# Newton steps of three inverse square roots moved from GpSimd to VectorE, in a fused graph-attention and transformer kernel

## The reference, cut to what matters

```python
x = x + gat(gat(ctx_512, adj=layernorm(x)))      # 8 heads of 32, leaky relu, masked softmax, elu
```

```python
hidden = layernorm(x)
h = rmsnorm(hidden, attn_norm_w)
q, k, v = h @ q_w.T, h @ k_w.T, h @ v_w.T        # 16 query heads, 4 key/value heads of 128
q, k = rope(rmsnorm(q, q_norm_w)), rope(rmsnorm(k, k_norm_w))
hidden = hidden + causal_attention(q, k, v) @ o_w.T
h2 = rmsnorm(hidden, ffn_norm_w)                 # then 8 experts of 176, top 2 by softmax(h2 @ gate_w.T)
out = x + hidden + sum_e combine_e * (silu(h2 @ wg_e.T) * (h2 @ wu_e.T)) @ wd_e.T
```

## Time and profile before

| what | us |
|---|---|
| median of 3 runs (lowest to highest) | 663.96 (662.97 to 664.13) |
| the profiled execution | 662.46 |
| its span | 660.7 |
| TensorE busy | 606.6 (92%) |
| VectorE busy | 434.6 (66%) |
| GpSimd busy | 305.9 (46%) |
| ScalarE busy | 268.6 (41%) |

### The profile page before, as it was taken

One profiled execution on the slowest core, in us unless ns is written; L12 is line 12 of the kernel. 1 busy time (PEld: TensorE's weight loads), 2 busy tenths in 40 slices (PEclk: granted clock), 3 DMA queues, 4 the chain that ended last, 5 costly groups with the idle time before them and its releaser, 6 DMA issues.

```text
span 660.7 us, 10362 instructions
## 1 busy us (share of the span) xinstructions
PE 606.6 (92%) x3271; PEld 437.0 (66%) x3271; DVE 434.6 (66%) x1279; ACT 268.6 (41%) x653; POOL 305.9 (46%) x588
## 2 busy tenths in 40 slices
PE   3799899489799999989799999989999998999998
PEld 2278468236586789736597789746768873666886
DVE  4997499389756387689757387655653656664463
ACT  2462563065566333055556333036750204675020
POOL 1493594278853240268854150267730027863000
PEclk9999899799999999998989999999999999999999
DMA  8920000000000000000000000000000000000000
GB/s 276 387 73 2 1 1 4 12 4 2 1 1 0 1 2 1 24 9 1 0 2 1 0 1 1 3 15 1 1 1 0 1 9 8 1 0 1 1 0 17
DMA packets 8729, 14.41 MB, mean 22 GB/s; under 512 B 908, under 2 KB 7372, under 8 KB 8420
## 3 DMA queue, kind: packets, MB, share of 16 engines
q1 hardware_dynamic: 8676, 13.76, 5.9%
HBM read 12.70 MB, written 1.05 MB: 21 GB/s over the span
## 4 chain that ended last, share of the span: by engine, by line
PE 64%; DVE 20%; issue 6%; POOL 4%; ACT 4%; DMA 1%; DVEq 0%; POOLq 0%; SPq 0%; ACTq 0%
PE bank L615 14%; PE bank L513 10%; PE bank L573 6%; PE bank L559 5%; PE bank L592 4%; PE ob L487 4%; PE tb L476 3%; PE bank L637 2%; DVE tt L958 2%; PE bank L588 2%; PE bank L584 2%; DVE ssq L1023 2%; ACT prob L726 2%; DVE m L1020 2%; DVE qT L958 1%
## 5 line engine op out<-in xcount | busy, mean ns | idle before, releaser
L559 PE MATMUL bank<-wqkv_sb,hT 128*128 128x512 f32 x192 | 95.0, 635 | 0.4 <-ACT v_sb L702 0.4
L726 ACT ACTIVATE prob<-bank,sneg,rms 128x128 f32<-128x128 f32 (+1 forms) x128 | 63.9, 508 | 59.6 <-DVE sneg L1052 59.4
L836 POOL TENSOR_TENSOR m<-early,rope_s 128x256 f32<-128x256 f32 x80 | 73.5, 942 | 30.8 <-ACT early L707 30.6
L513 PE MATMUL bank<-m,wgu_sb 128*128 128x128 f32 (+1 forms) x480 | 85.6, 329 | 0.8 <-DVE early L1099 0.8
L794 POOL TENSOR_SCALAR tt<-tt,gmn 128x256 f32<-128x256 f32 x96 | 67.3, 710 | 37.4 <-DVE gmn L958 37.0
L852 POOL TENSOR_SCALAR prob<-prob,srcp 128x128 f32<-128x128 f32 (+1 forms) x128 | 53.1, 432 | 51.4 <-DVE srcp L1123 51.2
L513 PEld LDWEIGHTS bank<-m,wgu_sb 128*128 128x128 f32 x480 | 71.0, 191 | 9.0 <-DVE early L1099 2.2
L573 PE MATMUL bank<-kT,qT 128*128 128x128 f32 (+1 forms) x256 | 61.5, 356 | 1.8 <-ACT prob L726 1.8
L559 PEld LDWEIGHTS bank<-wqkv_sb,hT 128*128 128x128 f32 x192 | 35.9, 199 | 36.9 <-issue 34.0
L615 PE MATMUL bank<-wo_sb,qT 128*128 128x256 f32 x256 | 59.0, 382 | 0.7 <-ACT qT L732 0.7
L707 ACT ACTIVATE early<-bank 128x512 f32<-128x512 f32 x40 | 24.1, 602 | 84.4 <-PE bank L559 84.4
(11 more groups left out here) (200 smaller groups left out, 1217.0 us busy)
## 6 DMA issues: line engine op xcount, KB each, us to landing
wqkv_sb<-wqkv_dram SPq DMA_DIRECT2D x1, 3072.0 KB, 12.0
wgu_sb<-wgu_dram SPq DMA_DIRECT2D x2, 1408.0 KB, 11.5
wo_sb<-wo_dram SPq DMA_DIRECT2D x1, 2048.0 KB, 18.2
wd_sb<-wd_dram SPq DMA_DIRECT2D x1, 1408.0 KB, 15.6
out_dram<-rows SPq DMA_DIRECT2D x8, 128.0 KB, 1.7
xin<-x_dram SPq DMA_DIRECT2D x3, 256.0 KB, 2.7
rows<-gat_rows_dram SPq DMA_DIRECT2D x2, 256.0 KB, 2.8
kT<-x_dram SPq DMA_DIRECT2D x1, 256.0 KB, 4.5
```

Source lines behind the costliest of these rows:

```text
L513: mm = pe.matmul(ps[:, m * N + c0:m * N + c1], wgu_sb[:, m, k, n * P:(n + 1) * P], tokT[:, k, c0:c1], start=(k == 0), stop=(k == KT - 1))
L559: mm = pe.matmul(ps[:, :], hT[:, k, t * P:(t + 1) * P], wqkv_sb[:, k, c * G * HD:(c + 1) * G * HD], start=(k == 0), stop=(k == KT - 1))
L726: ins = act.activation(prob[:, n % 5, i * nk:(i + 1) * nk], ps[:, i * nk:(i + 1) * nk], ACT.Exp, bias=sneg[:, n, i:i + 1], scale=rq(g, t, ...
L836: ins = pool.tensor_tensor(dst[:, :, c, :], src[:, :, 1 - c, :], s_, ALU.mult)
```

## The change

The three Newton steps of the row norms and of the normalisation ahead of a batch are done by VectorE, with the three-instruction form that the mask's root already uses. GpSimd's `link`, `link_a`, `newton` and `inverse_rms` go, and the semaphores `ln_seed`, `seed_ready`, `pool_a`, `pool_b` with them. `rms_ready` is left for the two groups of queries. `N_B = 94` only counts VectorE's own waits.

```diff
 # GpSimd
                 if a == LN2_AT[1]:
-                    pool.wait_ge(ln_seed, b + 1)
+                    pool.wait_ge(ln_ready, b + 1)
                     pool.nop(nofuse=True)
-                    for _ in range(3):
-                        newton(link_a, b, ln_y[:, :], ln_a[:, :], ln_v[:, :])
-                    pool.sem_inc(ln_ready, 1)
...
-                    if u in (1, 5, 9):
-                        inverse_rms(b, (u - 1) // 4)
 # VectorE, prep
                     first_guess(link_a, b, ln_y[:, :], ln_a[:, :], ln_v[:, :])
-                    dve.sem_inc(ln_seed, 1)
+                    for _ in range(3):
+                        newton(link_a, b, ln_y[:, :], ln_a[:, :], ln_v[:, :])
+                    dve.sem_inc(ln_ready, 1)
                 if a == LN2_AT[2]:
-                    dve.wait_ge(ln_ready, b + 1)
-                    dve.nop(nofuse=True)
 # VectorE, after the sum of squares of u = 1, 5, 9
-                        dve.tensor_scalar(y.bitcast(I32), a.bitcast(I32), -1, MAGIC, ALU.mult, ALU.add).then_inc(seed_ready, 1)
+                        link_b(b, dve.tensor_scalar(y.bitcast(I32), a.bitcast(I32), -1, MAGIC, ALU.mult, ALU.add))
+                        for _ in range(3):
+                            newton(link_b, b, y, a, v)
+                        if u > 1:
+                            dve.tensor_scalar(y, y, SCALE, None, ALU.mult).then_inc(rms_ready, 1)
 # VectorE, ahead of L1041
-                    dve.wait_ge(rms_ready, b * 3 + 1)
 # VectorE, score pieces 0 and 6
-                        dve.wait_ge(rms_ready, b * 3 + 2 + n // 6)
+                        dve.wait_ge(rms_ready, b * 2 + 1 + n // 6)
```

More of the change, by code:

```diff
@@ L72, in constants @@
     return c, spread
-N_B, N_P = 64, 36
+N_B = 94
 STEPS = 48
@@ L307, in block_program @@
         dve_a = sem("dve_a")
-        hn_ready, ln_seed, pool_a, ln_ready, hid_ready = sem("hn_ready"), sem("ln_seed"), sem("pool_a"), sem("ln_ready"), sem("hid_ready")
+        hn_ready, ln_ready, hid_ready = sem("hn_ready"), sem("ln_ready"), sem("hid_ready")
         def two(name):
@@ L325, in block_program @@
         raw_ready, m1_ready, m2_ready = sem("raw_ready"), sem("m1_ready"), sem("m2_ready")
-        k_ready, seed_ready, rms_ready, pool_b = sem("k_ready"), sem("seed_ready"), sem("rms_ready"), sem("pool_b")
+        k_ready, rms_ready = sem("k_ready"), sem("rms_ready")
         sneg_ready, srcp_ready, prob_ready = sem("sneg_ready"), sem("srcp_ready"), sem("prob_ready")
@@ L755, in _ @@
         def _(pool):
[L756 to L776, removed]
             def gat(b, a):
@@ L809, in prep @@
                     ins.then_inc(hid_ready, 1)
[L811 to L822, removed]
             def part(b, w):
```

## The result

| | before | after |
|---|---|---|
| median (lowest to highest), us | 663.91 (662.97 to 664.13), 4 runs | 680.09 (678.20 to 681.34), 4 runs |
| the profiled execution, us | 662.46 | 680.14 |
| its span, us | 660.7 | 678.3 |
| TensorE, VectorE, GpSimd, ScalarE busy, us | 606.6, 434.6, 305.9, 268.6 | 612.6, 462.2, 251.8, 268.7 |
| mean granted clock of TensorE | 0.977 | 0.965 |

Ratio 1.0244, 95% interval 1.0218 to 1.027: slower, as forecast, and 0.1 us from the predicted 680.0. That remainder is TensorE's work at the clock it was granted and, in both kernels, some 2.9 us of idle time that no group of waits lists (660.7 - 606.6 - 51.2, and 678.3 - 612.6 - 62.9). The 17.6 us of the two profiled executions are 11.7 of waits and 5.9 of the rest.

The account below looks back on a forecast made before the run. The prediction took TensorE, 64% of the chain that ended last, as the bound. Its terms, -2.0 + 1.5 - 2.0 + 8.8 + 1.4 + 8.0 + 1.0 = +16.7 us, gave 680 us, range 669 to 689.

Parts of the forecast that it names:

- Ahead of batch 0: Gap from the guess to the next VectorE instruction shrinks from 3.87 to 1.8 us, TensorE standing still: -2.0 us.
- L1001 at 122.4: Sign of being right: the VectorE instruction behind the steps ahead of the first batch starts at 122.4 us.
- Ahead of batches 1 to 3: Nine steps delay L1110, whose bank TensorE's L615 needs; 1.3 of 1.8 us covered: +0.5 three times, +1.5 us.
- Keys of batches 2 and 3: Key roots: L1041 starts 1.3 us earlier, but a GpSimd product may get in front of one: -1.0 each, -2.0 us.
- Keys and first roots of batches 0 and 1: Key and first query roots: VectorE has no slack, so the row maximum and TensorE come later: +4.2 and +4.6, +8.8 us.
- The exclusion: Long GpSimd instructions cost VectorE instructions beside them about 0.5 us: +0.8 from `pair_r`, +1.0 from L836, in batches 0 and 1.
- First roots of batches 2 and 3: First query roots: 0.4 us early without GpSimd's interference, +1.0 with two of its instructions in the way: +0.7 each, +1.4 us.
- Second roots: Second query roots, all batches: ten steps in front of score pieces 1 and 2, nothing covers: +2.0 four times, +8.0 us.
- Clock: TensorE's granted clock, batches 2 and 3: +1.8 at second query roots, -0.8 at keys; net +1.0, between -1.8 and +5 us.
- VectorE's busy time: Sign of being right: VectorE's busy time over the execution up by 25 to 35 us.
- TensorE's idle time: Sign of being right: TensorE's idle time over the execution up by 12 to 18 us.
- the round trip: Rival, all moved places: VectorE's slack takes the steps, only GpSimd's waits go: -7.4 us, 656.6; chance 0.06.

Follow-up runs that it names:

- the faster kernel: Against the kernel before, only the roots ahead of batch 0 and the key roots of batches 2 and 3 moved to VectorE: 660.86 us, ratio 0.9938.

## Why the prediction was right, and where its terms were off

- **Ahead of batch 0:** -2.0 predicted; the wait went from 7.3 to 5.3 us, and the gap behind the guess from 3.87 to 1.92. The sign "L1001 at 122.4" failed all the same, for the 1.95 us lost ahead of it.
- **Ahead of batches 1 to 3:** +0.5 three times; L615 waits 0.5 us three times, 1.6 in all, for the very instruction named.
- **Keys of batches 2 and 3:** -1.0 each; TensorE waits 0.9 us less in both. L1005 starts 1.3 us earlier behind its guess than L1041 did, and GpSimd's product did get in front of one multiplication.
- **Keys and first roots of batches 0 and 1:** +4.2 and +4.6; at L567 TensorE is 3.35 us later in batch 0 (174.65 against 171.30) and 3.6 in batch 1 (331.64 against 321.47, less the 6.57 by which it comes late to that batch's keys). Waits are 2.97 and 2.95 of that; the rest is the clock, counted again below. The exclusion was mis-sized. GpSimd's four `pair_r` instructions (138.49 to 140.71 in batch 0) lie on top of the new steps as foreseen, but the eleven steps between 138.56 and 141.36 take 2.8 us instead of 2.2: 0.6 us lost and not 2.0. L1005, freed of them, takes 1.29 instead of 2.54, as reckoned. So that part of the exchange was a gain of 0.65 us and not a loss of 0.8. The two-input product did catch two steps, of the masks' root (0.66 and 0.65 us at 142.15 and 142.84), which is the +1.0 of the prediction, at another place.
- **First roots of batches 2 and 3:** +0.7 each; +0.97 and +0.96 in TensorE's waits at L567, three of the ten steps in batch 2 taking 0.63 to 0.73 us. The page SBUF — State Buffer of the Trainium skill, "Who interferes with whom", has two-input instructions of VectorE contend with GpSimd's reads, and `tensor_scalar`, in its two-port modes, with GpSimd; the 0.73, 0.65 and (L996) 0.63 us beside the product, and 0.18 with it held back, agree. (L1029, on which the prediction rested, has one SBUF input, so it bears on the second half of that rule and not on the first, which the prediction quoted.) Where it has the other engine blocked for the whole of an instruction, batch 0 shows less: beside the 48-partition `pair_r`, four instructions in 2.22 us, steps are lengthened by 0.16 us at most.
- **Second roots:** +2.0 four times, 8.0; by TensorE's start times 2.10 twice and 1.16 and 1.18 in batches 0 and 1, 6.5 in all. By themselves all four cost 2.1, with the other roots on GpSimd and with them moved. The difference is the gain for GpSimd's normalisation that the prediction left off the path: in the step ahead of these roots L949 and L958 took 1.10 and 0.94 us with GpSimd's late products beside them, and L910 and L919 (173.08, 173.69) take 0.69 and 0.42 once that backlog is gone. The experiment with only these roots moved, where the backlog stays, has the 2.1 us at L476 in batches 0 and 1 too, and the one with all but these roots moved has the 0.9 us by itself.
- **Clock:** +1.0 with +5 as the upper bound; 5.9 in the profiled pair. 1.95 of it fell ahead of the first moved instruction, where TensorE's work is the same in both kernels (granted clock 0.96 against 0.98 there); among the profiled executions of the experiments this stretch had 0.96, 0.98 or 1.00, whatever they changed. That part no list of waits could give. The other 4 us are mis-sized by the list of places: I counted the clock at batches 2 and 3 alone, and it fell by more behind the second roots of batch 0 and the two long waits of batch 1.

In waits the terms were 15.7 us and came to 11.7; the clock's term was 1.0 and came to 5.9. The predicted time is as near as 0.1 us because these two cancel, not because each was right: that is luck. The direction, the places and most prices were right, and the largest single error is the +8.8 of batches 0 and 1, of which 5.9 came as waits. Of the signs put down, VectorE's busy time (+27.6 us) lies in its range; TensorE's idle time (+11.6) lies just under 12 to 18; and three steps were longer than 0.3 us, which was to be a sign of being wrong and is the exclusion that the same prediction had priced. Of the rivals, the round trip (656.6) is refuted as a description of the change and right as a description of three of its sixteen places (four groups in four batches), which is what made the faster kernel.

Open: why the granted clock falls so much more often with the second roots alone on VectorE (0.955) than with all roots there (0.965) while its waits are shorter (60.4 us in the execution of 684.44 against 62.9). The trace shows where some 5 us of it went, in the middle of stretches without any wait, and not why. Nor does any experiment move the first query roots alone; their price is read from the waits of the changed kernel.

## What to carry to other kernels

An instruction's price is set by its place in its queue: ten steps of 0.2 us cost 2.1 us each time in front of an instruction that another engine waits for, and nothing that the waits show (55.3 against 55.2 us) three score pieces later. Move only the round trips that somebody waits for, one place at a time, and compare each place's wait before and after. Add up the waits of the bounding engine and set them against the span: what is left over shows the clock's share, which in the profiled pair was a third of the loss (and a third of that third the luck of the pair) and, in two experiments, most of it. Compare executions of the same mean clock before a gain of a few us is credited to a change.

## What the runs showed of the hardware

- Dependent small VectorE steps start 0.20 us (128x2 and 128x8) to 0.21 us (128x16) apart, semaphore wait included; the same chain on GpSimd, ahead of batch 0 before, had twelve steps 0.30 us apart (120.80 to 124.11).
- One kernel's executions spread with the mean granted clock: the kernel before, in one series of 16, took 659.9 to 660.0 us at 0.982, 662.9 at 0.977, 663.9 to 664.7 at 0.974, 664.9 to 665.4 at 0.972 and 668.2 to 668.3 at 0.966. A change worth 1 us is smaller than this spread, and is read from the waits of a trace.
- A kernel whose waits add up to less than another's can be slower in the execution profiled, by the clock alone: with the key roots alone on VectorE 50.2 us of waits in 668.93 us, in the kernel before 51.2 in 662.46.
- The granted clock can fall with TensorE busy: to 0.51 over 7 us behind 60 us without a gap, in an execution of 684.44 us; the execution of 676.68 us of the same kernel has 1.00 there. It also falls while TensorE is idle: 0.80 over 4 us with 0.00 us of work (after, 144 to 148 us).
